# Entry of a chunk's tokens into a two-stack attention and feed-forward kernel: its place in the lists of GpSimd, ScalarE and TensorE

## What is computed

```
x = x + 0.5 * ffn_ref(layernorm(x), ...)      # stack 0: 6 layers
x = x + attn_ref(layernorm(x), ...)           # gated convolution and selective scan, 16 states
x = x + 0.5 * ffn_ref(layernorm(x), ...)      # stack 1: the same 6 layers, the same weights

def ffn_ref(x, ...):
    for i in range(6):
        x = attn_layer(shift_tokens(x), Wqkv[i], q_scale[i], k_scale[i], Wo[i]) + x
        x = ffn_layer(shift_tokens(x), ln_g[i], ln_b[i], W1[i], b1[i], W2[i], b2[i]) + x
    return x
```

## Time and profile before

| | |
|---|---|
| median of three runs | 3349.46 us (3340.23 to 3356.64) |
| the profiled execution, its own time | 3321.07 us |
| its span, first to last instruction | 3319.3 us |
| mean granted TensorE clock | 0.946 |
| DVE busy | 2903.0 us (87%) |
| PE busy | 2881.9 us (87%) |
| POOL busy | 2419.8 us (73%) |
| ACT busy | 2061.6 us (62%) |

### The profile page before, as it was taken

One profiled execution on the slowest core, in us unless ns is written; L12 is line 12 of the kernel. 1 busy time (PEld: TensorE's weight loads), 2 busy tenths in 40 slices (PEclk: granted clock), 3 DMA queues, 4 the chain that ended last, 5 costly groups with the idle time before them and its releaser, 6 DMA issues. The chain is left out here.

```text
span 3319.3 us, 132032 instructions
## 1 busy us (share of the span) xinstructions
PE 2881.9 (87%) x57914; PEld 1834.8 (55%) x57914; DVE 2903.0 (87%) x4216; ACT 2061.6 (62%) x3820; POOL 2419.8 (73%) x1687
## 2 busy tenths in 40 slices
PE   5788998989999989987777788998999988988987
PEld 3455565655565656553334455665665555565653
DVE  6789999989999999986897789989999988899984
ACT  3466666666566666665774466666676666566663
POOL 3677788787787787774464677788787787787873
PEclk8889999999999999998888899999999999999998
DMA  5233343333343333320002233333343332342330
GB/s 137 67 81 78 76 99 70 90 88 72 86 96 72 87 87 79 84 71 29 10 4 69 66 84 75 82 93 70 86 97 72 85 93 66 82 96 66 92 72 15
DMA packets 114725, 250.84 MB, mean 76 GB/s; under 512 B 27244, under 2 KB 60648, under 8 KB 114152
## 3 DMA queue, kind: packets, MB, share of 16 engines
q1 hardware_dynamic: 114152, 242.40, 30.8%
HBM read 37.82 MB, written 3.15 MB: 12 GB/s over the span
## 5 line engine op out<-in xcount | busy, mean ns | idle before, releaser
L1096 ACT ACTIVATE squares<-general 128x512 f32<-128x512 f32 x768 | 454.0, 597 | 686.8 <-PE general L661 677.7
L1290 POOL TENSOR_TENSOR probs<-probs,row_sum 128x1024 f32<-128x1024 f32 x192 | 365.4, 1903 | 427.7 <-DVE row_sum L968 427.7
L1270 POOL TENSOR_TENSOR q_ring<-q_ring,partner 128x512 f32<-128x512 f32 x384 | 491.4, 1280 | 198.6 <-DMA partner<-sines 198.0
L881 DVE TENSOR_TENSOR sines<-general,layer_tables 128x512 f32<-128x512 f32 x768 | 516.0, 672 | 76.8 <-ACT squares L1096 74.0
L1270 POOL TENSOR_TENSOR k_ring<-k_ring,partner 128x512 f32<-128x512 f32 x384 | 490.8, 1278 | 0.0
L659 PE MATMUL general<-xs_hi,wqkv_lo 128*128 128x512 f32 x768 | 454.1, 591 | 17.2 <-DVE xs_lo L908 8.0
L695 PE MATMUL general<-probs_t,v_buf 32*64 32x64 f32 x24576 | 336.6, 235 | 151.9 <-issue 79.5
L695 PEld LDWEIGHTS general<-probs_t,v_buf 32*64 32x64 f32 x24576 | 303.4, 134 | 241.3 <-issue 233.8
L1284 POOL TENSOR_TENSOR probs<-probs,q_scale 128x1024 f32<-128x1024 f32 x192 | 365.4, 1903 | 15.1
L671 PE MATMUL general<-att,wo 128*128 128x512 f32 x768 | 367.3, 623 | 5.4 <-ACT att L1166 5.4
L1276 POOL TENSOR_TENSOR probs<-probs,row_max 128x1024 f32<-128x1024 f32 x192 | 366.5, 1909 | 0.0
(11 more groups left out here) (233 smaller groups left out, 6317.1 us busy)
## 6 DMA issues: line engine op xcount, KB each, us to landing
partner<-sines SPq DMA_DIRECT2D x1536, 128.0 KB, 2.3
wqkv_raw<-in_wqkv SPq DMA_DIRECT2D x80, 208.0 KB, 2.7
wo<-in_wo SPq DMA_DIRECT2D x12, 512.0 KB, 5.1
w<-in_w SPq DMA_DIRECT2D x12, 341.0 KB, 3.2
base_dram<-x SPq DMA_DIRECT2D x8, 256.0 KB, 2.4
att<-in_wqkv SPq DMA_DIRECT2D x2, 1024.0 KB, 6.5
sines<-base_dram SPq DMA_DIRECT2D x8, 256.0 KB, 4.0
w<-in_w SPq DMA_DIRECT2D x12, 128.0 KB
```

What stands on the lines that cost most here:

```text
L881: e.tensor_tensor(by_seq(sines[:, i % 2, which, :]), g, both(layer_tables[:, 2 * which + 1, :]), ALU.mult).then_inc(S[f"sin_{side}"], 1)
L1096: e.activation(squares[:, (2 * p + which) % 4, :], general_of(("proj", k, n, p, which))[:, :], ACT.Square).then_inc(S[f"squared_{side}"], 1)
L1270: e.tensor_tensor(y, y, partner[:, i % 2, which, :], ALU.add).then_inc(S[f"rotated_{side}"], 1)
L1290: e.tensor_tensor(y, y, spread_keys(row_sum[:, i % 2, :]), ALU.mult).then_inc(S["probs_done"], 1)
```

## The change

In the substeps of an entry, GpSimd's part (`pool_enter`) now stands first, before the subtraction and the rotations; it stood between the normalisation of the probabilities and the rotation of k. TensorE's part (`pe_enter`) stands behind the keys' projection, where it stood ahead of it, and `Banks` hands out its banks in the same order. ScalarE's part (`act_enter`) stands in the source ahead of the shift of item `out_last`. All else in the diff gives plan entries names of their own, with the same lags (`PROBS_LAG` 12 is `EXP_LAG`, `shift` is `out_last`, `hidden` is `values_of`, and so on), and writes the lags as numbers (SUBSTEPS is 8).

```
@@ Banks.stack @@
+            if st.now:
+                n, p = st.now
+                self.use(("proj", k, n, p, 1), "cos_k", (g + n) * PAIRS + p + 1)
             if st.enter and st.enter[1] == 0:
                 self.norm(("enter", k, st.enter[0]))
             if st.enter and st.enter[1] == 1:
                 self.var(("enter", k, st.enter[0]))
-            if st.now:
-                n, p = st.now
-                self.use(("proj", k, n, p, 1), "cos_k", (g + n) * PAIRS + p + 1)
@@ tensor_stack @@
+                if st.now:
+                    pe_project(e, w, k, *st.now, 1)
                 if st.enter:
                     pe_enter(e, w, k, *st.enter)
-                if st.now:
-                    pe_project(e, w, k, *st.now, 1)
                 if st.values:
@@ scalar_stack @@
-                if st.out_last is not None:
-                    n = st.out_last
+                if st.enter:
+                    act_enter(e, w, k, *st.enter)
+                if st.shift is not None:
+                    n = st.shift
                     w.wait_ge(S["att_added"], (k * ITEMS + n) * 2 + 2)
...
                     act_shift(e, w, n % CHUNKS, 0)
-                if st.enter:
-                    act_enter(e, w, k, *st.enter)
@@ gpsimd_stack @@
             for st in PLAN:
+                if st.enter:
+                    pool_enter(e, w, k, *st.enter)
                 if st.off:
                     pool_sub(e, w, k, *st.off)
...
                 if st.added:
                     pool_rotate(e, w, k, *st.added, 0)
-                if st.exps:
-                    pool_probs(e, w, k, *st.exps)
-                if st.enter:
-                    pool_enter(e, w, k, *st.enter)
+                if st.probs:
+                    pool_probs(e, w, k, *st.probs)
                 if st.added:
                     pool_rotate(e, w, k, *st.added, 1)
```

More of the change, by code:

```diff
@@ L34 @@
 POOL_BANKS = 7
-SCORES_LAG = SUBSTEPS + 2
-SCORES_REST_LAG = SCORES_LAG
-SCALE_LAG = SCORES_LAG
-OFF_LAG = SCORES_LAG + 1
-EXP_LAG = SCORES_LAG + 2
-TURN_LAG = SCORES_LAG + 3
-VALUES_LAG = SCORES_LAG + 4
-VALUES_REST_LAG = SCORES_LAG + 4
-KEPT_LAG = SCORES_LAG + 4
+SCORES_LAG = 10
+SCORES_REST_LAG = 10
+SCALE_LAG = 10
+OFF_LAG = 11
+EXP_LAG = 12
+PROBS_LAG = 12
+TURN_LAG = 13
+VALUES_LAG = 14
+VALUES_REST_LAG = 14
+KEPT_LAG = 14
 V_LAG = 1
-SPREAD_LAG = SCORES_LAG
+SPREAD_LAG = 10
 PROBS = 2
@@ L108, in __init__ @@
         self.exps = self.group(t, EXP_LAG)
+        self.probs = self.group(t, PROBS_LAG)
         self.turn = self.group(t, TURN_LAG)
@@ L120, in __init__ @@
         self.spread = self.group(t, SPREAD_LAG)
-        self.out_first = next(((self.item(t, at), i) for i, at in ((0, 17),) if self.item(t, at) is not None), None)
+        self.out_first = self.item(t, 17)
+        self.first_added = self.item(t, 17)
         self.out_last = self.item(t, 21)
+        self.last_added = self.item(t, 21)
+        self.shift = self.item(t, 21)
         self.center = self.item(t, 22)
         self.var = self.item(t, 23)
+        self.var_turn = self.item(t, 23)
         self.root = self.item(t, 24)
         self.gates = self.item(t, 25)
+        self.gelus = self.item(t, 25)
         self.values_of = next(((self.item(t, at), js) for at, js in ((26, (0,)), (27, (1, 2))) if self.item(t, at) is not None), None)
+        self.hidden = next(((self.item(t, at), js) for at, js in ((26, (0,)), (27, (1, 2))) if self.item(t, at) is not None), None)
         self.ffn_out = self.item(t, 28)
+        self.ffn_added = self.item(t, 28)
+        self.ffn_shift = self.item(t, 28)
         self.load = (n // CHUNKS + 1, p) if self.now and n % CHUNKS == CHUNKS - 1 and n // CHUNKS + 1 < DEPTH else None
@@ L509, in macaron_kernel @@
             for st in PLAN:
-                for key in (("att", k, st.out_last), ("ffn", k, st.ffn_out), ("enter", k, st.enter[0] if st.enter and st.enter[1] == 2 else None)):
+                for key in (("att", k, st.shift), ("ffn", k, st.ffn_shift), ("enter", k, st.enter[0] if st.enter and st.enter[1] == 2 else None)):
                     if key[2] is not None and key[2] not in (range(ITEMS - CHUNKS, ITEMS) if key[0] == "ffn" else ()):
@@ L787, in tensor_stack @@
                     pe_spread(e, w, k, *st.spread)
-                if st.out_first:
-                    pe_out(e, w, k, *st.out_first)
+                if st.out_first is not None:
+                    pe_out(e, w, k, st.out_first, 0)
                 if st.scores:
@@ L1008, in vector_stack @@
                     dve_scores(e, w, k, *st.scale)
-                if st.var is not None:
-                    dve_var(e, w, ("ffn", k, st.var))
-                if st.out_last is not None:
-                    dve_out(e, w, k, st.out_last, 1)
-                if st.values_of:
-                    for j in st.values_of[1]:
-                        dve_hidden(e, w, k, st.values_of[0], j)
+                if st.var_turn is not None:
+                    dve_var(e, w, ("ffn", k, st.var_turn))
+                if st.last_added is not None:
+                    dve_out(e, w, k, st.last_added, 1)
+                if st.hidden:
+                    for j in st.hidden[1]:
+                        dve_hidden(e, w, k, st.hidden[0], j)
                 if st.norms_back is not None:
@@ L1222, in scalar_stack @@
                     act_shift(e, w, n % CHUNKS, 0)
-                if st.enter:
-                    act_enter(e, w, k, *st.enter)
-                if st.ffn_out is not None and st.ffn_out < ITEMS - CHUNKS:
-                    n = st.ffn_out
+                if st.ffn_shift is not None and st.ffn_shift < ITEMS - CHUNKS:
+                    n = st.ffn_shift
                     w.wait_ge(S["ffn_added"], k * ITEMS + n + 1)
```

18 lines of the change are left out of this document (8 added, 10 removed).

## The result

The changed kernel takes 3309.62 us (median of 7 runs, 3301.59 to 3322.14) against 3346.47 us for the kernel before (7 runs, 3328.83 to 3356.64): a ratio of 0.9906, 95% interval 0.9882 to 0.993, so 0.94% faster, which is 31.5 us of 3346.47. The two medians themselves lie 36.9 us apart; the interval, 23.4 to 39.5 us, holds both. The forecast of 3320 us was 10 us too slow and its range holds the time. Some 3 us of the 10 are the starting point: the forecast started from the median of three runs, 3349.46 us. The profiled execution of the changed kernel took 3307.77 us, with a span of 3306.0.

What follows compares the result with a forecast made beforehand. VectorE and TensorE, nearly full, bound the body; at chunk entries all engines wait for one another. Terms of 14.2 and 15.3 us per stack, together 29.5, off the 3349.5 us median gave 3320 us, range 3303 to 3341.

Steps and rivals of the forecast that it cites:

- C: Chunk 2, stages 0 and 1 (t = 10, 11): keys' projection covers TensorE's wait for the square; 1.7 and 1.3 us.
- E: Chunk 3, stages 0 and 1 (t = 18, 19): square starts earlier, keys' projection ahead of var; 2.0 and 2.5 us.
- A: Chunk 1, stages 0 and 1 (t = 2, 3): earlier square, keys' projection fills TensorE's idle time; 3.3 us per stack.
- B: Chunk 1, stage 2 (t = 4): GpSimd's scale starts at rstd's end, ahead of a rotation; 2.0 us per stack.
- D: Chunk 2, stage 2 (t = 12): scale ahead of the probabilities removes VectorE's wait before the sines; 4.1 us per stack.
- F: Chunk 3, stage 2 (t = 20): as at t = 12, but limited by TensorE's output passes; 1.1 and 2.1 us.
- clock rival: Chunk entries: shorter TensorE idleness may keep its clock at 2.4 GHz; 9 us more gain, 3311 us; chance 0.08.
- collision rival: VectorE's addition of epsilon meets moved GpSimd work on shared ports; 10.6 us lost, 3331 us; chance 0.08.
- slower rival: GpSimd's q rotations wait behind the entry work and delay scores or DMA; 38 us lost, 3358 to 3378; chance 0.05.
- absorbed: Only the engine that was ahead gains and the body eats it; gain 10 us, 3340 us; chance 0.17.

Runs made afterwards that it cites:

- e2: Kernel before with only GpSimd's entry part moved first in its substep: 3298.61 us, ratio 0.9906 to the kernel before.
- e9: Kernel before with only GpSimd's square (stage 0) moved first in its substep: 3323.42 against 3342.1 us, ratio 0.9951.
- e5: Kernel before with only GpSimd's scale (stage 2) moved first in its substep: 3330.26 against 3341.89 us, ratio 0.9964.
- e7: Changed kernel with ScalarE's stage 2 root and its centred copy also moved early: 3286.79 us against the kernel before's 3341.89, ratio 0.983.
- e11: The kernel before, word for word, run for one more trace: single execution of 3346.46 us.

## Why the prediction was right, and where not

**The mechanism was right.** The main trace marks that it named are there: the scale right behind rstd, the 4.07 us gone, var behind the keys' projection, a wait for the output projection at t = 21. Two marks came out otherwise. ScalarE's wait before its shift is 2.19 us, not under 1, because it waits through rstd's transposition and the scale themselves. And the lead of the pair of profiled executions was 15.0 us at the addition of t = 21 (forecast 14), but -1.6 at the norm transposition of item 23 and 13 at the end of the program, not 29. By its own words a lead that shrinks was a sign of being wrong.

**Most of that shrinking lead is scatter.** The profiled execution of before has the shortest first body of its four traces (1268.07 us), that of after met 1284.78: 16.7 us of difference in a stretch in which nothing is moved, with TensorE busy for 12.7 us more at a lower clock. The prediction held the gains to be kept to the end. The ratios bear this out to within a few microseconds, for they are near what the entries alone give: 37.5 of 3346.5 us make 0.9888 (measured 0.9906, interval from 0.9882), 31.6 of 3334.9 for e2 0.9905 (0.9906), 15.9 of 3342.1 for e9 0.9952 (0.9951), 17.4 of 3341.9 for e5 0.9948 (0.9964), 60.8 of 3341.9 for e7 0.9818 (0.983). The measured advantage is the smaller one more often than not, by 6 us at most, so that a few microseconds are given back in the body is not excluded.

**The weak step is "I take the sum, since each term is the smaller of the two engines' waits".** The sum was 29.5 us and the entries gave 37.5: the terms were mis-sized, most of all C and E (1.7 / 1.3 forecast against 2.8 / 3.1, and 2.0 / 2.5 against 3.7 / 4.7). But not all of the 8.0 us is that step. The trace that the prediction was read from has the shortest entries of the four, 350.7 us against a mean of 354.2. Against that one trace the gain is 34.0 us, and the terms come out, first and second stack, as A 3.4 / 3.0, B 1.8 / 2.0, C 1.9 / 1.6, D 4.9 / 5.1, E 2.3 / 4.4 and F 1.7 / 1.8. So C was sized well for that trace, and E in its first stack; 3.5 of the 8.0 us come from reading one trace, and they lie in C and in E of the first stack, where the same program's length goes with the granted clock (above). The 4.5 us that are left lie mostly in D (0.8 and 1.0), in E of the second stack (1.9) and in F of the first (0.6). There several waits follow one another in a stretch, and it fits that a start moved by 2 us shortens more than the one wait that was read: in e9 VectorE's idle time in E fell by 4.1 us. This is an argument and not a test of each wait. The smaller of two waits that meet in one row was no bound here.

**The clock rival is true in part.** The granted clock over the whole first entry, of the kernel before and of the changed kernel, by windows:

```profile
17.69:179.55 161.86, 112.64 (x1663) 73.31 (x1667) 118.39 (x188) 70.19 (x142) 88.27 (x63) 0.81 0.35 84
```

```profile
18.26:164.51 146.25, 108.11 (x1655) 71.06 (x1656) 120.48 (x188) 70.95 (x142) 89.30 (x64) 0.85 0.39 92
```

It rose from 0.81 to 0.85, and TensorE was busy for 4.5 us less. The other traces agree: 0.81 to 0.82 in the order of before and 0.85 in all three of the changed kernel, and 0.83 to 0.86 against 0.87 to 0.89 in the second entry. But the place on which the rival rested most, the output passes of t = 21, shows no gain on average. In the first stack they take 5.65, 5.29, 5.29 and 3.59 us in the four traces of the order of before and 5.88, 4.66 and 4.35 in the three of the changed kernel (means 4.96 and 4.96); in the second 5.11, 5.08, 5.29 and 4.43 against 5.73, 4.54 and 4.36 (4.98 and 4.88). How much of the gain beyond the sum is the clock's stays open. No run moves the clock and leaves the order alone, but the scatter of one program shows the size: 3.4 us in C and 2.4 in E of the first stack.

**The collision rival is true in kind and small in size.** VectorE's addition of epsilon, of the kernel before and of the changed kernel, all 56 of them (busy us, mean ns):

```profile
L849 DVE TENSOR_SCALAR norm_t<-norm_t 128x16 f32<-128x16 f32 x56 | 20.0, 357 | 1.9
```

```profile
L858 DVE TENSOR_SCALAR norm_t<-norm_t 128x16 f32<-128x16 f32 x56 | 22.3, 398 | 1.9
```

2.3 us more, against the 10.6 us of the rival: three of the six of t = 3, 11 and 19 grew by 0.75 to 1.3 us and one shrank by 0.6. The growth is no scatter: the 56 take 18.5 to 20.3 us in the four traces of the order of before and 21.4 to 22.8 in the three of the changed kernel. The instruction of t = 11 takes 1.46 us (above), from 84.45 to 85.91, and GpSimd's subtraction beside it ends at 85.88. The Trainium skill's rule in "SBUF — State Buffer", section "Who interferes with whom", has the direction right, and the trace agrees with 0.18 us at the least and 1.46 at t = 11. How often an instruction meets its neighbour depends on the order.

**The slower rival didn't come.** The q rotation of t = 12 stands 1.2 us behind the scale's start and is long done when its k rotation ends; no score waits for it. In *absorbed* the time would have been 3340; A, C, E and F, which it had struck out, gave 23.9 of the 37.5 us.

## What to carry to other kernels

Where engines take their instructions in order and wait for each other in turn, look for a short instruction whose reader idles while it stands behind work that nobody needs yet. Here that was worth 0.9%, and 1.7% once the wait that was left (for ScalarE's root and centred copy) was treated in the same way. The second figure holds four activation-table loads less on ScalarE besides the order. Measure the gain as the stretch between two fixed instructions, and read that stretch in more than one execution before a term is sized from it: here the same stretch of 29 us took 32.7 at a lower granted clock, both entries together repeat to 2%, and a body of 1270 us differs by 20. Do the parts by themselves: in a chain two moves may need each other (A), and their gains need not add up.

## What was not expected of the hardware

- The granted TensorE clock differs between executions of the same program: 0.96 to 0.98 in stretches of nearly equal work, and the stretch is 1266.8 to 1290.2 us long with it. VectorE is busy for 1170 to 1172 us in the four shown, and for 1166 to 1175 in all 28.
- The same eight passes of the output projection at t = 21 take 3.59 to 5.65 us in the first stack of one and the same order of instructions, that of before, and 3.60 us in e7. The idle time just ahead of the projection in front of them doesn't decide it: TensorE stood idle there for 2.03 us in the kernel before (5.65 us) and for 1.90 us in e11 (3.59 us). The passes of e11, and the places around them by windows in the changed kernel, e7 and e11:

```profile
174.35 3.59 PE L671 MATMUL general<-att,wo 128*128 128x512 f32 x8
```

```profile
155.21:164.51 9.30, 7.36 (x13) 3.77 (x14) 6.04 (x9) 2.34 (x4) 7.88 (x6) 0.63 0.25 56
```

```profile
145.56:153.54 7.98, 7.98 (x89) 5.55 (x81) 6.01 (x10) 3.74 (x9) 7.49 (x6) 0.79 0.30 68
```

```profile
171.60:181.74 10.14, 7.32 (x26) 3.27 (x25) 6.05 (x10) 2.34 (x4) 6.22 (x4) 0.98 0.23 52
```

  The granted clock there is 0.63, 0.79 and 0.98; the first two are a mixture of the two levels, 1.2 and 2.4 GHz, and the third is nearly all the upper one.
